# GpSimd's first subtraction waits for both row maxima of the first block instead of for its sixteen transposes

## The reference, cut to what matters

```python
def _L0_xattn_ref(query, key):          # query (1, 256, 2048), key (1, 25088, 2048)
    a = jnp.einsum('bqd,bkd->bqk', query, key)
    e = jax.nn.softmax(a, axis=-1)
    c = jnp.einsum('bqk,bkd->bqd', e, key)
    return c
...
x = x + _L0_xattn_ref(_layernorm(x, axis=-1), ctx_4096)
x = x + _L0_attn_ref(_layernorm(x, axis=-1), ...)
x = x + _L0_ffn_ref(_layernorm(x, axis=-1), ...)
```

## Time and profile before

| what | value |
|---|---|
| median of three runs | 2432.33 us |
| the profiled execution's own time | 2430.85 us |
| its span in the trace | 2429.3 us |
| TensorE busy | 2395.9 us (99%) |
| VectorE busy | 2000.1 us (82%) |
| GpSimd busy | 1422.6 us (59%) |
| ScalarE busy | 1098.9 us (45%) |

### The profile page before, as it was taken

How to read it: one execution, slowest core, us unless ns; L and a number is a source line. 1 busy time by engine, 2 the same in 40 slices (tenths; PEclk the granted TensorE clock), 3 DMA queues, 4 the chain that set the end, 5 groups by cost and what they waited for, 6 DMA issues and landing times.

```text
span 2429.3 us, 35962 instructions
## 1 busy us (share of the span) xinstructions
PE 2395.9 (99%) x11078; PEld 1967.5 (81%) x11078; DVE 2000.1 (82%) x2798; ACT 1098.9 (45%) x1577; POOL 1422.6 (59%) x1052
## 2 busy tenths in 40 slices
PE   6999999999999999999999999999999999999999
PEld 5888888888888888888888888888888888777777
DVE  8888888888888888888888888888888888874466
ACT  5444444444444444444444444444444444433553
POOL 2766666666666665565665556566565566561551
PEclk9999999999999999999999999999999999999999
DMA  9998989999899989999989998999999998889743
GB/s 235 258 244 226 249 219 247 235 227 241 225 247 237 231 224 239 237 222 231 238 228 235 229 226 224 243 227 220 240 235 225 239 234 226 209 192 200 181 131 101
DMA packets 487287, 543.93 MB, mean 224 GB/s; under 512 B 72902, under 2 KB 361670, under 8 KB 484808
## 3 DMA queue, kind: packets, MB, share of 16 engines
q1 hardware_dynamic: 477256, 501.37, 85.0%
q0 software_dynamic: 9984, 41.95, 5.3%
HBM read 488.71 MB, written 30.41 MB: 214 GB/s over the span
## 4 chain that ended last, share of the span: by engine, by line
PE 90%; DVE 3%; DMA 2%; issue 1%; SPq 1%; ACT 1%; POOL 0%; DVEq 0%; ACTq 0%
PE ps L1519 30%; PE ps L1520 29%; PE ps L1521 29%; DMA quads<-probs 2%; SPq L495 1%; PE ps L1547 0%; DVE ch_lo L1104 0%; DVE tr L1100 0%; DMA tr<-wt_dram 0%; DVE acc L1239 0%; PE ps L1528 0%; PE ps L1752 0%; DVE probs L1157 0%; DMA x_in<-in_x_dram 0%; PE ps L1821 0%
## 5 line engine op out<-in xcount | busy, mean ns | idle before, releaser
L635 POOL TENSOR_TENSOR nat_lo<-raw,nat_hi 128x512 fp32r<-128x512 f32 x784 | 1185.7, 1543 | 815.7 <-ACT nat_hi L795 779.7
L1104 DVE TENSOR_TENSOR ch_lo<-tr,ch_hi 128x512 fp32r<-128x512 f32 x784 | 807.6, 1030 | 236.4 <-ACT ch_hi L784 234.9
L784 ACT CAST ch_hi<-tr 128x512 fp32r<-128x512 f32 x784 | 476.6, 620 | 709.6 <-PE ps L1521 655.2
L1519 PE MATMUL ps<-ch_hi,xt_hi 128*128 128x512 f32 x1696 | 666.2, 393 | 9.3 <-DVE ch_lo L1104 8.0
L1520 PE MATMUL ps<-ch_lo,xt_hi 128*128 128x512 f32 x1696 | 661.3, 390 | 0.0
L1521 PE MATMUL ps<-ch_hi,xt_lo 128*128 128x512 f32 x1696 | 661.3, 390 | 0.0
L1519 PE MATMUL ps<-nat_hi,pt_hi 128*128 128x512 f32 x1568 | 610.3, 389 | 0.0
L1520 PE MATMUL ps<-nat_lo,pt_hi 128*128 128x512 f32 x1568 | 610.1, 389 | 0.0
L1521 PE MATMUL ps<-nat_hi,pt_lo 128*128 128x512 f32 x1568 | 610.0, 389 | 0.0
L1100 DVE STREAM_TRANSPOSE tr<-quart 128x512 f32<-128x512 f32 x784 | 548.5, 700 | 0.9 <-DMA quart<-in_ctx_dram 0.9
L795 ACT CAST nat_hi<-raw 128x2048 fp32r<-128x2048 f32 x196 | 374.4, 1910 | 203.0 <-PE ps L1521 190.1
(11 more groups left out here) (205 smaller groups left out, 1248.6 us busy)
## 6 DMA issues: line engine op xcount, KB each, us to landing
quart<-in_ctx_dram SPq DMA_DIRECT2D x392, 512.0 KB, 8.5
raw<-in_ctx_dram SPq DMA_DIRECT2D x196, 1024.0 KB, 9.2
quads<-probs SPq DMA_DIRECT2D x368, 64.0 KB, 2.9
wq_in<-in_L_attn_Wq_dram POOLq DMA_DIRECT2D x16, 1024.0 KB, 6.4
win<-in_L_ffn_W_base_dram SPq DMA_DIRECT2D x64, 256.0 KB, 12.6
tr<-wt_dram POOLq DMA_DIRECT2D x64, 256.0 KB, 3.6
wt_dram<-stage SPq DMA_DIRECT2D x32, 256.0 KB, 5.7
wt_dram<-stage_b SPq DMA_DIRECT2D x32, 256.0 KB, 10.6
```

What stands on the lines that cost most here:

```text
L635: last = pool.tensor_tensor(nat_lo[:, j, t], raw[:, j % 2, t], nat_hi[:, j, t].bitcast(F32), ALU.subtract)
L784: act.copy(ch_hi[:, c % RING_CH, :], tr[:, c % RING_TR, :]).then_inc(chunk_hi, 1)
L1104: dve.tensor_tensor(ch_lo[:, c % RING_CH, :], tr[:, c % RING_TR, :], ch_hi[:, c % RING_CH, :].bitcast(F32), ALU.subtract).then_inc(chunk_s ...
L1519: pe.matmul(out_, a_hi, b_hi, start=start, stop=False)
```

## The change

GpSimd's stream waits once before the first block's four pieces. Before, it waits until VectorE has transposed all 16 chunks of block 0 (that frees `quart0`, where `nat_lo` lies). After, it waits until `max_ready` is at 2 * 1 + 2 = 4, that is until both maxima of the second turn are there. These come on VectorE behind all transposes of block 0, so the memory is free then too.

```diff
@@ -641,7 +641,7 @@
             w4 = wq_in[:].rearrange("p (n j) -> p n j", j=REP)
 
-            pool.wait_ge(chunk_transposed, DC)
+            pool.wait_ge(max_ready, START[0].times(TT, TT))
             split_block(FIRST)
             with pool.Fori(0, WQ_PAIRS) as i:
```

## The result

The changed kernel takes 2440.91 us (median of seven runs, 2437.49 to 2442.74), the kernel before, run beside it, 2433.31 (seven runs, 2429.74 to 2436.77). The ratio is 1.003 with a 95% interval of 1.002 to 1.0039: slower by 5 to 9.5 us. The forecast was 2433.3 with 2428.2 to 2437.5 around it, and 0.07 for "slower". It was wrong.

What follows compares the result with a forecast made beforehand. TensorE's work plus its gaps was taken as the bound, busy 2395.9 of 2429.3 us. A sum of +1.0 us on 2430.85 gave 2431.9; with the runs' median 1.5 us higher, the forecast was 2433.3, range 2428.2 to 2437.5.

Steps and rivals of the forecast that it cites:

- GpSimd's start: Second turn: GpSimd starts subtracting at 49.7 us instead of 45.08, once the second maximum is there; bounds 49.4 and 52.3.
- The first gap: TensorE before chunk 3, second turn: the 2.36 us gap and its slow clock go, up to 4.1 us saved.
- What is late next: Second turn, chunk 6: a 3.4 us gap and 1.7 us of slow clock put piece 0 at 63.3, +1.0 us.
- The argument that nothing issued later could hold up the older half: Block 1's second half, issued before the raw piece of 51.06, cannot be delayed by it; landing stays near 57.1.
- Raw piece 2: Block 0's load, issued at 55.9 instead of 51.06, lands at 61.3 to 61.7, or 64.2; free of cost.
- 4 us to spare: Claimed slack at chunk 9 of the second turn, behind ScalarE's rounding of raw piece 2.
- SP's queue: Block 2's first half, issued from 62.5 to 65.1, lands at 75.5; VectorE may wait 1 us, free of cost.
- Behind it everything is paced by TensorE, and the lateness dies out: GpSimd's later pieces: 1.9 of 3.6 us slack used at the third turn's chunk 4, then no further cost.
- the lateness is handed on: Rival: late rows reach TensorE through ScalarE, in part or in full; 7.2 us in full, 2439.5 us; chance 0.12.
- its second leg: The rival's same chain returning at chunk 4 of the third turn, where only 3.6 us are to spare.
- the signs of being wrong: Chunk 8's transpose well before 56 (gain up to 4 us), or TensorE waiting at chunk 9 or third turn's chunk 4.

Runs made afterwards that it cites:

- e17: Changed kernel, block 0's raw pieces 2 and 3 in memory of their own, loads issued about when the kernel before issued them: 2435.3 us, 1.0009 times before.
- e19: e17 without the gates on raw pieces 0 and 1 of block 1, so these are issued earlier: 1.0012 times before.
- e3: Changed kernel, raw piece 2 of block 0 in memory of its own and issued at 44.9 us: 1.0042 times before.
- e5: Kernel before, with block 2's first half issued between raw pieces 2 and 3 of block 0: 1.0047 times before.
- e9: Changed kernel, raw pieces 2 and 3 of block 0 in memory of their own, issued together with the maxima: 1.002 times before.
- e11: Changed kernel with a milder wait, GpSimd waiting for 20 transposes; it started at 45.4 us: 1.0001 times before.
- e15: Kernel before, ScalarE rounding block 1's row pieces 0 and 1, and the third turn's 2 and 3, behind later chunks: 1.0031 times before.
- e18: Kernel before (old GpSimd wait) with the same memory and load gates as e17: 2434.13 us, 1.0006 times before.
- e21: e17, with GpSimd starting block 1's row piece 2 in the third turn only after the softmax denominators' update: 2436.8 us, 1.0006 times before.
- e14: Changed kernel, ScalarE rounding block 1's row pieces 0 and 1, and the third turn's 2 and 3, behind later chunks: 1.0029 times before.

## Why the prediction was wrong, step by step

1. GpSimd's start: right. 50.07 for 49.7, and `neg_max` alone takes 0.16 us (forecast: most of 1.76 for two lost beside GpSimd).
2. The first gap: half right. 1.10 us is left of 2.36. ScalarE had `ch_hi` of chunk 3 at 50.2, later than I took it, and GpSimd's start fell on its `ch_lo` (1.64 us). The clock stayed at 1.00.
3. What is late next: right place, wrong size. The gap in front of chunk 6 came, ended by `ch_lo`, with VectorE waiting for the load (56.73). It was 1.05 us, not 3.4, since TensorE was ready for chunk 6 at 57.2 and not at 55.5, and no slow clock followed. Piece 0: 61.45 for 63.3. The sum here was -0.9, not +1.0. The argument that nothing issued later could hold up the older half is refuted by the change itself. The last load of the half, issue to landing, before (raw piece 2 follows at 51.06) and in the change (nothing follows until 56.47):

```profile
quart<-in_ctx_dram SPq DMA_DIRECT2D x1, 512.0 KB, 15.3
```
```profile
quart<-in_ctx_dram SPq DMA_DIRECT2D x1, 512.0 KB, 14.0
```

It landed near the forecast 57.1 all the same, because in this execution it was issued 0.9 us later (42.6 for 41.7). That is luck. The Trainium skill's rule of ring order (DMA: Bandwidth & Descriptors, Queues, rings and completion order) is not contradicted in its words, since it speaks of taking descriptors; my conclusion on the landing is.
4. Raw piece 2: right, 5.0 us to land, no gap at chunk 9. The "4 us to spare" do not follow from the figures beside them, which give 5.2 with a load of 5.4 us and 2.7 with one of 8.3; nothing hung on it.
5. SP's queue: issue right (62.8), landing 79.2 for 75.5. I took the median of four quarter loads, 10.4, for the last one, which took 14.4 both before (59.7 to 74.1) and in the change (64.8 to 79.2). VectorE's wait of 4.6 us, forecast as 1, opened no gap on TensorE in the second turn (which reaches chunk 14 at 85 by the forecast's own terms, not at 84.6); its share in the late maxima of the third (+4.7 us) was not separated.
6. "Behind it everything is paced by TensorE, and the lateness dies out": this is the step that failed, in two terms. Raw piece 0 of block 1 was to land 8.6 us behind its issue; behind the late half it took 13.8, and block 1's first subtractions started at 85.2, not 80.5. And the slack of the third turn was read at chunk 4, 3.6 us. The tight place is chunk 6, behind the split of the probabilities, with 0.8 us. And piece 7, which the forecast does not name, had a gap too. Two gaps of 2.2 and 2.4 us and two slow stretches of 1.7 each stand where the sum has nothing.

The rival that came true is "the lateness is handed on", by its second leg, though at piece 7 and chunk 6 of the third turn and not at the chunks 9 and 4 that it and the signs of being wrong name. Its price, 7.2 us and 2439.5, is near the measured 7.3 to 7.6 us, but by luck: it prices a start 7.2 us late handed on one for one, while the start was 5.0 us late, and 3.4 us of the loss are two slow stretches that it does not contain. I gave it 0.12, on the strength of a slack read at the wrong chunk.

What stays open: how the 2.2 us that e17 leaves divide between its late raw piece 2, the overlap and chance is not shown, since its interval (0.2 to 4.4 us) is as wide as the rest. How the older half is held up by younger loads is not shown either. A version that beats the kernel before was not found.

## What to carry to other kernels

A late start on an engine that is off the critical path is priced by the loads that its buffers release, and then by every load queued behind these: follow the lateness around the ring of buffers until a place absorbs it, for at least two blocks. Slack is the smallest over all consumers behind the late item, not that of the next one. Look for holes in a DMA queue that is else full: here the engines' busy share fell to 0.50 from 52.5 to 57, with 1.12 behind the second gap, and the loads that came behind the hole landed 5 to 7 us late. In e19 the queue gave nothing back: raw piece 0 issued 7.6 us earlier than in e17 was rounded at 78.59, not before e17's 77.93.

## What the runs showed of the hardware that I had not expected

- A load lands later when a younger one follows it soon in the same queue. The last 512 KB load of block 1's second half, issued at 41.5 to 43.6, took 15.1 to 15.8 us in the ten kernels in which a raw piece follows by 53.2 us (before, e3, e5, e9, e11, e15, e17, e18, e19, e21). It took 13.5 to 14.5 us in the nine in which the next load comes at 53.3 or later.
- A VectorE operation with two inputs on 128x1 or 128x2 takes 0.14 to 0.16 us in nearly all its executions before, and 0.58 to 1.24 us in the five that meet GpSimd's subtractions. In the changed kernel one of the six that meet them still takes 0.14.
- Gaps of 1.05 and 1.10 us left TensorE's clock at 1.00. Gaps of 2.17, 2.36 and 2.43 us were followed by the 1.2 GHz level. The length of the gap does not settle it: behind 2.48 us in e17 the mean of the next 4.5 us is 1.00, behind 2.30 us in e21 it is 0.66 over 5. In e14 it is 0.66 behind a gap of 1.89 us and 1.00 behind one of 2.99. What else decides over a slow stretch, worth some 1.7 us each time, is not shown here:

```profile
142.00:147.00 5.00, 4.76 (x14) 3.84 (x15) 2.34 (x5) 2.94 (x3) 0.07 (x1) 0.66 0.88 266
155.00:160.00 5.00, 4.69 (x21) 3.89 (x22) 5.00 (x7) 1.24 (x2) 4.87 (x4) 1.00 1.09 254
```
